# A deformable-convolution block: gathers read pairs of pixels laid out before launch, and batch norm's constants are worked out later

## The reference

```
out_normal = conv(x, w_normal)
offset     = concat(conv(x, w_offx), conv(x, w_offy))        # 18 channels: 9 taps, dy and dx
out_x      = deform_conv(x, offset, w_dx)
out_y      = deform_conv(x, offset, w_dy)
out = relu(bn1(conv(concat(out_normal, out_x, out_y), w_fusion)))
return relu(bn2(conv(out, w_conv2)) + x)
```

## Time and profile before

| what | value |
|---|---|
| median of 3 runs | 2737.38 us (2736.04 to 2740.46) |
| profiled execution, span from the first to the last instruction | 2989.8 us |
| profiled execution's own time around that span | not given with these runs |
| PE busy, share of the span | 2685.1 us, 90% |
| ACT, DVE, POOL busy | 67%, 62%, 63% |
| granted TensorE clock, mean over the span | 0.983 |
| gathers (q0, software) | 471.97 MB, 53.7% of 16 DMA engines |
| SP's DMAs (q1, hardware) | 104.06 MB, 10.5% |
| chain that ended last | PE 61%, ACT 13%, DVE 9%, issue 8%, unknown 7%, DMA 2% |

### The profile page before, as it was taken

How to read it: one execution, slowest core, us unless ns; L and a number is a source line. 1 busy time by engine, 2 the same in 40 slices (tenths; PEclk the granted TensorE clock), 3 DMA queues, 4 the chain that set the end, 5 groups by cost and what they waited for, 6 DMA issues and landing times.

```text
span 2989.8 us, 51480 instructions
## 1 busy us (share of the span) xinstructions
PE 2685.1 (90%) x17840; PEld 2612.5 (87%) x17840; DVE 1849.5 (62%) x4940; ACT 2004.2 (67%) x4925; POOL 1870.2 (63%) x1806
## 2 busy tenths in 40 slices
PE   1558899998999999999999999999999999999999
PEld 1458889998999998999899999999999999999999
DVE  3566666666666666666666666666666666666640
ACT  2566677776767676777677677776676776767741
POOL 3666666666666666666666666666666666666620
PEclk9789999999999999999999999999999999999999
DMA  9676667666666666666666767766666666666620
GB/s 278 202 231 193 206 200 220 202 208 198 205 205 201 198 208 199 201 206 205 204 204 203 215 209 219 215 181 186 183 186 183 181 182 186 186 182 185 179 90 23
DMA packets 218596, 579.32 MB, mean 194 GB/s; under 512 B 31840, under 2 KB 87264, under 8 KB 217952
## 3 DMA queue, kind: packets, MB, share of 16 engines
q0 software_dynamic: 144000, 471.97, 53.7%
q1 hardware_dynamic: 74336, 104.06, 10.5%
HBM read 562.80 MB, written 69.73 MB: 212 GB/s over the span
## 4 chain that ended last, share of the span: by engine, by line
PE 61%; ACT 13%; DVE 9%; issue 8%; another core or an unknown queue 7%; DMA 2%; POOL 1%; ACTq 0%; SPq 0%; POOLq 0%
PE work L363 13%; PE work L369 13%; PE work L366 13%; ACT mixed L495 5%; PE turned L395 5%; PE acc L369 5%; PE acc L366 5%; PE acc L363 5%; ACT samp L495 3%; DVE mixed L700 3%; PE work L348 2%; DVE feat L659 2%; DMA cell_table<-in_xpix 2%; DVE samp L706 2%
## 5 line engine op out<-in xcount | busy, mean ns | idle before, releaser
L318 POOL DMA_INDIRECT cells<-cell_table,index x1800 | 1859.0, 1033 | 1002.6 <-issue 390.4
L495 ACT ACTIVATE mixed<-cells,wgt 128x256 f32<-128x256 f32 x1800 | 758.0, 498 | 29.7 <-DMA cells<-cell_table,index 20.8
L495 ACT ACTIVATE samp<-mixed,wgt 128x128 f32<-128x128 f32 x1800 | 623.1, 396 | 205.6 <-issue 103.6
L700 DVE SCALAR_TENSOR_TENSOR mixed<-cells,wgt,mixed 128x256 f32<-128x256 f32 x1800 | 744.8, 478 | 21.8 <-ACT mixed L495 16.5
L363 PE MATMUL work<-feat,w_hi 128*128 128x320 f32 x2160 | 694.0, 321 | 13.7 <-issue 10.0
L369 PE MATMUL work<-feat,w_lo 128*128 128x320 f32 x2160 | 678.1, 314 | 10.9 <-issue 10.4
L366 PE MATMUL work<-feat,w_hi 128*128 128x320 f32 x2160 | 677.2, 314 | 7.4 <-issue 7.1
L706 DVE SCALAR_TENSOR_TENSOR samp<-mixed,wgt,samp 128x128 f32<-128x128 f32 x1800 | 512.0, 346 | 62.0 <-ACT samp L495 34.3
L659 DVE TENSOR_TENSOR samp_lo<-turned,samp_hi 128x640 fp32r<-128x640 f32 x360 | 295.8, 822 | 393.0 <-ACT samp_hi L494 329.2
L494 ACT ACTIVATE samp_hi<-turned 128x640 fp32r<-128x640 f32 x360 | 250.9, 697 | 374.3 <-remote 265.1
L363 PE MATMUL acc<-samp_hi,w_hi 128*128 128x320 f32 x1440 | 451.0, 313 | 11.9 <-issue 7.0
(11 more groups left out here) (70 smaller groups left out, 3199.4 us busy)
## 6 DMA issues: line engine op xcount, KB each, us to landing
cell_table<-in_xpix SPq DMA_DIRECT2D x54, 768.0 KB
cells<-cell_table,index POOLq DMA_INDIRECT x1800
x_raw<-in_xflat SPq DMA_DIRECT2D x40, 410.0 KB
cell_table<-in_xpix SPq DMA_DIRECT2D x2, 6912.0 KB, 38.3
late<-in_x SPq DMA_DIRECT2D x40, 320.0 KB
out<-late SPq DMA_DIRECT2D x40, 320.0 KB
late<-in_weights SPq DMA_DIRECT2D x3, 1152.0 KB, 32.5
cells<-in_weights SPq DMA_DIRECT2D x1, 657.0 KB, 4.1
```

What stands on the lines that cost most here:

```text
L318: eng.indirect_dma_start(out=cells[:, g, :], out_offset=None, in_=table[0:(b + 1) * CELLS, :], in_offset=bass.IndirectOffsetOnAxis(ap=inde ...
L495: return eng.activation(dst, src, ACT.Copy, scale=scale)
L700: eng.scalar_tensor_tensor(out=mixed[:, tp, j], in0=cells[:, (k * TILES + j) % GSLOTS, 2 * C:4 * C], scalar=wgt[:, par, 1, 0, j, k:k + 1], ...
```

## The change

`kernel()` now lays out `in_xpair` on the host in place of `in_xpix`: row n holds pixel n and the pixel one image row below it, 1 KB. Two rows in succession, 2 KB, hold the four pixels of cell n, in the order upper left, lower left, upper right, lower right. The gather still brings 512 floats to each partition, from row n on. `cell_table`, `fill`, both of its semaphores and all waits for them are gone. ACT's `upper` and DVE's lower addition read their two pixels at a distance of 256 floats, where they were side by side. The batch norm chain stands behind `samples_low(0, 0)` on DVE, and the square root behind `upper(2, ...)` on ACT.

```
-            fill(0, CELLS, first_table)
             load_weights(1)
...
-                if fl.table:
-                    at_least(eng, table_part, 32 * i)
-                    fill(CELLS + i * PART, PART, table_part)
...
-                        out=cells[:, g, :], out_offset=None, in_=table[0:(b + 1) * CELLS, :],
+                        out=cells[:, g, :], out_offset=None, in_=xpair,
                         in_offset=bass.IndirectOffsetOnAxis(ap=index[:, par, j, k:k + 1], axis=0),
...
-            for b in range(B):
-                if b == 0:
-                    eng.wait_ge(first_table, 32)
-                else:
-                    eng.wait_ge(table_part, 32 * PARTS * b)
-                for c in range(b * STRIPS, (b + 1) * STRIPS):
-                    gather(c, c % 2, b)
+            for c in range(NS):
+                gather(c, c % 2)
...
+        corner = cells[:, :, :].rearrange("p g (x y c) -> p g x y c", x=2, y=2)
...
-                    copy(mixed[:, tp, j], cells[:, g, 0:2 * C], scale=wgt[:, par, 0, 0, j, k:k + 1])\
+                    copy(mixed[:, tp, j].rearrange("p (x c) -> p x c", x=2), corner[:, g, :, 0, :],
+                         scale=wgt[:, par, 0, 0, j, k:k + 1])\
...
+                    both = mixed[:, tp, j].rearrange("p (x c) -> p x c", x=2)
...
-                        out=mixed[:, tp, j], in0=cells[:, (k * TILES + j) % GSLOTS, 2 * C:4 * C],
+                        out=both, in0=corner[:, (k * TILES + j) % GSLOTS, :, 1, :],
...
-            eng.wait_ge(bn_step, 1)
-            eng.activation(root[:], var[:], ACT.Sqrt).then_inc(root_done, 1)
             weights_high(1)
...
             upper(2, 0, 2, 0, 0)
+            eng.wait_ge(bn_step, 1)
+            eng.activation(root[:], var[:], ACT.Sqrt).then_inc(root_done, 1)
             eng.wait_ge(bn_step, BN_STEPS)
...
-    xpix = np.ascontiguousarray(xflat.T)
+    xpix = xflat.T
+    rows = B * CELLS
+    xpair = np.concatenate([xpix[0:rows], xpix[PITCH:PITCH + rows]], axis=1)
```

More of the change, by code:

```diff
@@ L33 @@
 CELLS = 6912
[L34 to L38, removed]
+FLAT = B * CELLS + PITCH
+PAIR = 2 * C
+CELL = 2 * PAIR
+assert (H + 2 * LEAD - 1) * PITCH + 1 <= CELLS
 NORMAL, DEFX, DEFY, FUSE, SECOND = 0, 9, 18, 27, 54
@@ L96, with __init__ @@
 class Flags:
-    def __init__(self, i=None, table=True):
+    def __init__(self, i=None):
         mid = i is None
@@ L116, in __init__ @@
         self.weights = {} if mid else WEIGHTS_AT.get(i, {})
-        self.table = table if mid else i < (B - 1) * PARTS
     def has(self, job):
@@ L132, in at_least, with deform_block @@
     eng.wait_ge(sem, value)
-def deform_block(nc, x, xflat, xpix, weights, bn, const, out):
+def deform_block(nc, x, xflat, xpair, weights, bn, const, out):
     ctx = ExitStack()
@@ L142, in sem @@
             return ctx.enter_context(nc.semaphore(name))
-        table = nc.dram_tensor("cell_table", (B * CELLS, CELL), F32).ap()
         w_hi = sb("w_hi", [128, WCOLS], F32R)
@@ L202, in deform_block @@
         x_in, x_hi_done, x_lo_done = sem("x_in"), sem("x_hi_done"), sem("x_lo_done")
-        first_table, table_part = sem("first_table"), sem("table_part")
         o_done, o_out = sem("o_done"), sem("o_out")
@@ L248, in load_x @@
                 eng.dma_start(x_raw[:], xflat[:, bass.ds(start, SLOT)]).then_inc(x_in, 16)
[L250 to L255, removed]
             def load_weights(n):
@@ L298, in _ @@
                 eng.wait_ge(out_stored[par], 16 * (NS // 2))
-            eng.wait_ge(table_part, 32 * (B - 1) * PARTS)
         @block.gpsimd
@@ L307, in _, with gather @@
             eng.memset(mid[:].bitcast(F32), 0.0).then_inc(zeroed, 1)
-            def gather(c, par, b):
+            def gather(c, par):
                 at_least(eng, idx_ready, c + 1)
@@ L699, in sample @@
                     at_least(eng, upper_done, TILES * T + j + 1)
+                    both = mixed[:, tp, j].rearrange("p (x c) -> p x c", x=2)
                     eng.scalar_tensor_tensor(
-                        out=mixed[:, tp, j], in0=cells[:, (k * TILES + j) % GSLOTS, 2 * C:4 * C],
-                        scalar=wgt[:, par, 1, 0, j, k:k + 1], in1=mixed[:, tp, j], op0=ALU.mult, op1=ALU.add,
+                        out=both, in0=corner[:, (k * TILES + j) % GSLOTS, :, 1, :],
+                        scalar=wgt[:, par, 1, 0, j, k:k + 1], in1=both, op0=ALU.mult, op1=ALU.add,
                     ).then_inc(mixed_done, 1)
@@ L731, in _ @@
             x_low(0, 0)
+            eng.wait_ge(cst_in, 16)
+            indices(0, 0)
+            weights_low(1)
+            sample(0, 0, 0, 0)
+            x_low(1, 1)
+            sample(1, 1, 0, 1)
+            samples_low(0, 0)
             eng.wait_ge(bn_in, 16)
@@ L753, in _ @@
             assert steps[0] == BN_STEPS
[L754 to L760, removed]
             def step(i, par, fl):
@@ L852 @@
         img[:, LEAD:LEAD + H, 1:1 + W] = x[b]
-    xpix = np.ascontiguousarray(xflat.T)
+    xpix = xflat.T
+    rows = B * CELLS
+    xpair = np.concatenate([xpix[0:rows], xpix[PITCH:PITCH + rows]], axis=1)
     bn = np.stack([np.asarray(v) for v in (L0_conv_bn1_g, L0_conv_bn1_b, L0_conv_bn1_m, L0_conv_bn1_v,
                                            L0_conv_bn2_g, L0_conv_bn2_b, L0_conv_bn2_m, L0_conv_bn2_v)], axis=1)
-    arrays = {"x": np.ascontiguousarray(x.transpose(1, 0, 2, 3).reshape(C, B * H * W)), "xflat": xflat, "xpix": xpix,
+    arrays = {"x": np.ascontiguousarray(x.transpose(1, 0, 2, 3).reshape(C, B * H * W)), "xflat": xflat, "xpair": np.ascontiguousarray(xpair),
               "weights": np.ascontiguousarray(weights), "bn": np.ascontiguousarray(bn), "const": shape_constants()}
```

## The result

The changed kernel takes 2702.05 us (median of 4 runs, 2701.89 to 2705.56), the kernel before 2736.71 (4 runs, 2735.85 to 2740.46) beside it: ratio 0.9874, 95% interval 0.9859 to 0.9889. The forecast was 2702, with 2685 to 2714 as its range.

A forecast was written before the change was run, and what follows sets the result against it. PE was taken to be close to its bound in the middle, with time lost at the start. From 2737.4 us, 31 came off for the start and 4 for the other images' table DMAs: 2702 us, range 2685 to 2714.

The forecast's parts named there:

- The start: Before the first turn: the indices, not the table, end POOL's wait; first turn at 34.0, gain 31.1 us.
- The held gather: First gather on POOL, beside DVE's `w_lo`: held until 24.3 us; if no gather is held, the gain is 33.2.
- Does the shift last: After the start: both chains begin with the first gather, so its shift is passed on to later strips.
- The chain: Batch norm's new place in strip 0: third tap's turn 3.5 us late, hidden within the strip, taken as 0.
- PE's need and the middle: Middle strips: PE needs 62.8 us a strip, leaving 2.2 us idle that a relief there could give.
- the small DMAs' 4 us: Other images' tables: 27 steps lose two DMAs of 768 KB, 0.14 us a strip, 4 us for the median.
- the 85 us: PE's idle time in the 150 us from 60 on, where it has 65 us of work.
- B: Rival: the table DMAs do cost in the middle, 2692 us, at the very end 2647; chance 0.14.
- C: Rival: only part of the start comes through, table filled sooner unprofiled or chain replacing the wait, about 2720; chance 0.13.
- D: Rival: a partition's 2 KB moves in two pieces, POOL writes twice the descriptors, about 4100 us; chance 0.04.
- E: Rival: nothing measurable, what starts sooner waits elsewhere, 2735 us; chance 0.03.
- The other sum: Whole kernel under the profiler: 2989.8 less 31 for the start and 14 for the small table DMAs, 2945 us.

The follow-up runs named there:

- the two half changes: Changed kernel with the first image's two fill DMAs added again, unwaited: ratio 0.9982; kernel before with second weights and x issued ahead of the fill: ratio 1.0011.
- the other layout: Changed kernel with whole cells of 2 KB laid out before launch and operands side by side: 2703.00 us, ratio 0.9868.

## Why the prediction was right

**The start: right, with its mechanism.** The step said that the first gather leaves the table's wait for the index's, and that the first turn moves from 65.12 to 34.0. It came at 34.29 (33.23 in the second profile of the changed kernel). Against the second profile of before, where it is at 64.79, that is 30.5 us for the 31.1 forecast. I named both waits, the table's and the weights', and removed both in the sum. That each alone would have kept the start was not in the forecast; the two half changes showed it.

**The held gather: right.** The forecast held the first gather until 24.3; it ended at 24.04. The early split of the weights shows the cause: 1.09 instead of 2.61 us. The Trainium skill's inference, "SBUF — State Buffer", section "Who interferes with whom", that `tensor_tensor` does not stall descriptor generation, is not borne out here. One small term was missed: POOL starts 0.94 us behind the end of the index, where I had taken 0.11. It cost nothing, because `w_lo` held the gather anyway, and the indices were 0.3 sooner.

**Does the shift last: right.** The shift is 32.4 us at strip 1, 35.0 at strip 5, and 34.8 at strip 39.

**The chain: right.** The third turn was forecast 3.5 late and was 3.65 late; it was to be made good at 0.7 us or more a tap, within strip 0, and was, but for 0.5 us, after one tap. I charged it at 0, and no cost of it can be told from the noise. DVE stood idle for 4.63 us ahead of the chain's second link, close to the 5 forecast.

**PE's need and the middle: mis-sized, and its 4 us are put in the wrong place.** A strip needs 64.5 us, not 62.8. I took 0.147 us as the distance of all matmuls. That fits `acc` alone, with twelve distances in 1.76 us (1505.61 to 1507.37 in the changed kernel); `work`, with 270 of the 378, has 0.150 (the pair of the earlier trace rows writes `work` and is 0.15 apart), and behind five turns the second matmul comes later too. PE in the changed kernel:

```profile
1507.37 0.71 PE L372 MATMUL turned<-cst,samp 128*128 128x128 f32 x5
1507.84 0.40 PE L340 MATMUL work<-feat,w_hi 128*128 128x320 f32 x1
1508.07 0.31 PE L343 MATMUL work<-feat,w_hi 128*128 128x320 f32 x1
1508.22 0.32 PE L346 MATMUL work<-feat,w_lo 128*128 128x320 f32 x1
...
1510.47 0.31 PE L346 MATMUL work<-x_hi,w_lo 128*128 128x320 f32 x1
```

From 1508.22 to 1510.47 there are 15 distances, 0.150 each; from the turns to the second matmul it is 0.70 where my sum had 0.61. 270 x 0.003 and ten times 0.09 are 1.7 us. So the 2.2 us of idle time a strip, from which I scaled the small DMAs' 4 us, did not exist: in the middle they are worth 0.

Nor were the 85 us all idle that I took for it in the 150 us from 60 on: PE is busy for 83.54 us there, which leaves 66.5. My 65 us of work went by distances at a granted clock of 1.00, and the mean of that stretch is 0.83, between TensorE's two levels of 1.2 and 2.4 GHz. It is much the same in the later profiles: 0.80 in the kernel before from its first turn to 240 us, 0.77 in the changed one from its first turn to 180. What the lower clock costs at the start was not in the sum, and no run measures it apart.

The gain ahead of strip 5 is 35.0, 4 more than at the first turn; profiles without small DMAs scatter by as much there (strip 5 at 324.91 and 325.23 in the changed kernel, 329.75 with the other layout), so I can't say that the small DMAs made it. That the median came out to 0.1 us is in good part luck: 4 of the forecast's 35 us were put in the middle, which gave none, about as many came ahead of strip 5 from a cause that is not shown, and the changed kernel's own runs spread over 4 to 5 us.

**The rivals.** B falls: with the small DMAs and without, strips 5 to 39 take the same time. C falls as priced: the second profile has the first gather of before at 52.55, and the fill takes as long in an execution that agrees with the timed runs. D falls by the packet count and the median of 946 ns. E falls by the ratio. The other sum, 2945 us for the profiled span, missed by 245: the span is 2700.2. It carried on the 252 us, and the 14 of the small DMAs, that only the first profile of the kernel before has.

## What to carry to other kernels

Ask of each wait that you remove what else ends at the same time. Here the table that POOL waited for and the queue that it blocked for SP cost the same 30 us. With the wait gone and the queue blocked the gain was 0.2%; with the weights ahead in the queue and the wait kept the loss was 0.1%. And where PE is at its bound in the middle, only what moves its first real work counts; compare the profiled span with the timed median first, since a stall that only one profile shows is no price.

## What the runs showed of the hardware

A large DMA holds the issue of the next on the same queue: in the first profile of the kernel before the two fills' issue takes 19.68 us, and the weights' behind them 23.11; behind the fill that nothing waits for it takes 31.57. The same instruction takes 0.49 us in the changed kernel, where nothing large stands ahead.

A gather that begins beside `w_lo`, a `tensor_tensor` of 128x2304 with two inputs in SBUF, takes 2.3 to 3.2 us instead of 0.95 or 1.09, in every trace where the two meet, and ends 0.8 to 1.0 us behind it. It is not `tensor_tensor` alone. One of the longest gathers of the changed kernel begins beside the additions of `mixed` and `samp`, `scalar_tensor_tensor` with two inputs in SBUF, and ends 0.82 behind the last of these, at 371.48:

```profile
367.28 2.06 DVE L679 SCALAR_TENSOR_TENSOR mixed<-cells,wgt,mixed 128x256 f32<-128x256 f32 x5
367.77 3.71 POOL L301 DMA_INDIRECT cells<-in_xpair,index  x1 [0.30 <-DVE mixed L679]
369.26 1.40 DVE L685 SCALAR_TENSOR_TENSOR samp<-mixed,wgt,samp 128x128 f32<-128x128 f32 x5
```

Most gathers beside such additions are not held so, and no run shows why. Of the 952 gathers of this trace that begin beside neither these additions nor `w_lo` or `x_lo`, none takes more than 1.13 us.

POOL starts its first gather 0.94 us behind the end of DVE's index instruction, where that releases it. And a profile can be 9% slower than the timed runs of the same kernel, with "issue" and "unknown" making 15% of the chain that ended last; in the second profile of that kernel "issue" is 1% and "unknown" does not appear.
